# Quantising the last feed-forward's weights inside the preceding gated feed-forward, and a longer tile pipeline for the last one

## The chip, the cores and the metric

One NeuronCore of a Trainium2 chip runs one program. The metric is the device time of the program in microseconds (us); smaller is better. The engines are named as in the profile: PE is the matrix engine (PEld its weight loads), DVE the vector engine, ACT the scalar engine, POOL GpSimd, SP the engine that issues most of the DMAs.

## The reference, cut to what matters

Four layers, each an attention and a feed-forward with a residual, over an activation `x` of 4 x 512 x 256 in float32. The change touches the third layer's feed-forward (which keeps its own arithmetic), the start of the last attention, and the last feed-forward:

```python
# third layer's feed-forward, "L2_ffn": ternary weights, row scales s
h = silu(tlin(x, w1, s)) * tlin(x, w2, s)      # 256 -> 1024, gated
h = gelu(tlin(h, h1, s)); h = gelu(tlin(h, h2, s))   # 1024 -> 1024, twice
return tlin(h, w3, s)                          # 1024 -> 256

# last feed-forward, "L3_ffn": every operand is quantised to FP4 blocks
def fake_quant_nvfp4(x, global_scale):         # blocks of 16 along a row
    amax = max(abs(xb)); sc8 = fp8(clip(amax / 6 * global_scale, 0, 448))
    dq = sc8 / global_scale
    a = clip(abs(xb) / dq, 0, 6)
    return sign(xb) * nearest_fp4(a) * dq
def nvfp4_linear(x, w, s_in):
    s_w = 448 * 6 / max(abs(w))                # over the whole weight
    return fake_quant_nvfp4(x, s_in) @ fake_quant_nvfp4(w, s_w).T
hidden = silu(nvfp4_linear(x, gate_w, s_in)) * nvfp4_linear(x, up_w, s_in)
return nvfp4_linear(hidden, down_w, s_in_down)
```

`gate_w` and `up_w` are 1024 x 256, `down_w` is 256 x 1024.

## The kernel before

A Python program writes one list of steps, `plan`, and then five loops (one for each engine, `tensor_program`, `vector_program`, `scalar_program`, `gpsimd_program`, `sync_program`) walk that list; each engine takes its part of every step in the order of the list. So the place of a step in the list is its place in the queue of each engine that it uses. Waits are on semaphores, and `hold(latest_of_all(), ...)` at the end of a stage (`stage`) makes every engine wait for everything before.

**L2_ffn** works on two pairs of batches (1024 tokens each). For a pair it walks 40 weight blocks: 16 blocks of 256 x 128 for w1 and w2 in turn (the gated layer), 8 blocks of 1024 x 128 for h1, 8 for h2, and 8 for w3. `next_block` takes block n: it adds the split of block n+1 into a high and a low float32r part (`SplitBlock`: ACT copies the high part, L1916, DVE subtracts, L1761) and the load of block n+2 on SP. Then come the matmuls of the block (three passes, L1431) and a `HiddenTile` for each half of the tokens: ACT activation (L1919), in the gated layer DVE's product with the "up" half (L1765), ACT high copy (L1921), DVE low part (L1768). Two buffers each hold the raw blocks and the split ones. GpSimd does nothing in this stage, and the tile `XT` is unused.

**L3_xattn** begins with four weight loads and a 1 MB load of the context on SP, then a first batch's layer norm, whose square root stands in ACT's queue behind the copies of the turned context.

**L3_ffn** has two parts. First the weights: three loads of 1 MB and two scalars, then for gate, up and down in turn a `WeightScale` (DVE maximum of 128 x 2048, L1774; GpSimd `partition_all_reduce`, L2068; four tiny DVE operations), and the quantising of 128 x 2048 elements, whose result is turned by PE (16 transposes for each weight, L1588) and copied by ACT into `Gt`, `Ut`, `Dt` (bfloat16). A `hold` of all engines ends that part. Then the activations: `x_part(b)` normalises and quantises a batch (128 x 1024 elements), `hidden_part(t)` computes gate and up for a tile of 128 tokens (PE, ACT silu L1929, DVE product L1823), and `down_part(t)` quantises the hidden tile (128 x 1024), turns it, multiplies by `Dt` and adds to X (L1827), which is stored.

Quantising n elements is three pieces of work in the list. `Quantise`: DVE takes block maxima (L1787) and ten small operations in all on the n/16 block scales, each waiting for the one before, up to the inverse scales (L1807); then GpSimd multiplies the data by them (L2074). `RoundFp4`: DVE clips (L1811), masks the exponent (L1813), makes the grid step (L1816), adds and subtracts (L1818, L1820); then GpSimd multiplies by the scales into bfloat16 (L2082). `push` orders them so that the list has Quantise of item k, then RoundFp4 of item k-1, then the turning of item k-2. Two buffers hold y, q and the small scales; `Quantise` of item k waits for the GpSimd product of item k-2 (`y_free`). There is one `mg` buffer.

Of the kernel before, what the change touches and what calls it, by code (L numbers as in the profile page):

```python
# [8 lines left out]
P = 128  # L9
# [3 lines left out]
TB = S // P  # L13
# [111 lines left out]
WeightScale = namedtuple("WeightScale", "w col i s_in maxed reduced done")  # L125
Quantise = namedtuple("Quantise", "src n gs s after inv scaled")
RoundFp4 = namedtuple("RoundFp4", "s n after q_free rounded done")
# [16 lines left out]
def build_program(nc, dram, out):  # L144
    ctx = ExitStack()
    with ctx:
# [11 lines left out]
        def sem(event):  # L158
            return event.by.sem
# [48 lines left out]
        zero1 = sb(ctx, "zero1", [P, 1])  # L208

# [910 lines left out]
        def L2_ffn(scope):  # L1120
# [29 lines left out]
            n_block = [0]  # L1150

            def next_block():
# [74 lines left out]

            load_block(0)
# [5 lines left out]
            for pair in range(2):  # L1234
# [6 lines left out]
                e_out = output(pair, act[0], [e_h])  # L1241

# [17 lines left out]
        q4 = Stage()  # L1260

        def L3_ffn(scope):
            Gt, Ut = sb(scope, "L3f_GT", [P, KC, FF], BF16), sb(scope, "L3f_UT", [P, KC, FF], BF16)
            Dt = sb(scope, "L3f_DT", [P, KF, C], BF16)
            big = 2 * FF
            q4.y = [sb(scope, f"L3f_y{i}", [P, big]) for i in range(2)]
            q4.mg = sb(scope, "L3f_mg", [P, big])
            q4.qq = [sb(scope, f"L3f_q{i}", [P, big], BF16) for i in range(2)]
            q4.small = [sb(scope, f"L3f_small{i}", [P, 5, big // BLOCK]) for i in range(2)]
            col = sb(scope, "L3f_cols", [P, 12])  # L1270
            q_free, y_free, n_q = [None, None], [None, None], [0]

            def quantise(src, n, gs, after):
                s = n_q[0] % 2
                n_q[0] += 1
                st = Quantise(src, n, gs, s, [*after, y_free[s]], due("inverse_scales"), due("scaled"))
                add(st)
                return dict(s=s, n=n, read=st.scaled)

            def round_to_fp4(item):  # L1280
                s, n = item["s"], item["n"]
                st = RoundFp4(s, n, [item["read"]], q_free[s], due("fp4_rounded"), due("fp4_ready"))
                add(st)
                y_free[s] = st.done
                return s, q4.qq[s][:, 0:n], st.done

            half, whole = [], []

            def push(item, then):
                round_one()  # L1290
                half.append((item, then))

            def round_one():
                rounded = [(then, round_to_fp4(item)) for item, then in half]
                half.clear()
                for then, result in whole:
                    then(*result)
                whole[:] = rounded

            def flush():  # L1300
                round_one()
                round_one()

            def transposed(s, qo, pieces, dst, after, copy_after=()):
                for i in range(0, len(pieces), 4):
                    part = pieces[i:i + 4]
                    i_bank, bank = ALL.take()
                    st = Turn16(part, qo, bank.bitcast(BF16), [ALL.free[i_bank], *after], due("turned"), dst(i // 4),
                                list(copy_after), due("turned_out_scalar"))
                    add(st)  # L1310
                    ALL.free[i_bank] = st.done
                q_free[s] = st.mm
                return st.done

            with ExitStack() as inner:
                Wn = {n: sb(inner, f"L3f_{n}", [P, big]) for n in ("gate", "up", "down")}
                hold([
                    load(Wn["gate"][:, :].rearrange("p (m c) -> p m c", c=C), dram["L3_ffn_gate_w"].rearrange("(m p) c -> p m c", p=P)),
                    load(Wn["up"][:, :].rearrange("p (m c) -> p m c", c=C), dram["L3_ffn_up_w"].rearrange("(m p) c -> p m c", p=P)),
                    load(Wn["down"][:, :].rearrange("p (m c) -> p m c", c=FF), dram["L3_ffn_down_w"].rearrange("(m p) c -> p m c", p=P)),  # L1320
                    load(col[:, 10:11], dram["L3_ffn_s_in"].to_broadcast([P, 1])),
                    load(col[:, 11:12], dram["L3_ffn_s_in_down"].to_broadcast([P, 1]))])
                alpha = {}
                for i, (n, s_in) in enumerate((("gate", 10), ("up", 10), ("down", 11))):
                    g, al = col[:, 3 * i + 1:3 * i + 2], col[:, 3 * i + 2:3 * i + 3]
                    st = WeightScale(Wn[n][:, :], col, i, s_in, due("weight_max"), due("weight_max_all"), due("alpha_ready"))
                    add(st)
                    alpha[n] = al

# [846 lines left out]
```

## Time and profile before

| | us |
|---|---|
| median of three runs | 3914.71 (3909.6 to 3918.46) |
| the profiled execution | 3912.9 |
| its span in the trace | 3911.1 |
| DVE busy | 1951.7 (50%) |
| PE busy | 2835.9 (73%) |
| GpSimd busy | 1112.9 (28%) |

What lies around the span is 1.8 us. The rows are read so: a row of a timeline gives start, duration, engine, line, operation, output<-input with shapes, and in brackets the idle time of the engine before it and what ended it. A row of a table of windows gives the busy time of each engine in a stretch, with the number of instructions, the clock that PE was granted (1.00 is 2.4 GHz, 0.50 is 1.2 GHz), the busy share of the DMA engines and GB/s.

### The profile page before, as it was taken

The numbers are of one execution on the slowest core, as the hardware profiler recorded it, in microseconds if no ns is written. First come the engines' busy times: TensorE is split into PE (matmuls) and PEld (weight loads), VectorE is DVE, ScalarE is ACT, GpSimd is POOL, SyncE is SP. The second block draws the span as 40 slices with busy tenths as digits, with TensorE's granted clock in tenths as the row PEclk, the third lists the DMA queues.
The fourth block names the chain that finished last, engine by engine and source line by source line (L and its number), as shares of the span: only waits on it lengthen the run. The fifth ranks groups of instructions, "written<-read, shape, count | busy, mean of one in ns | idle before, by whom it ended". The sixth has DMA issues, their size and how long they took to land. (4 is left out here: it accounts for less than half of the span.)

```text
span 3911.1 us, 44194 instructions
## 1 busy us (share of the span) xinstructions
PE 2835.9 (73%) x16750; PEld 1614.4 (41%) x16756; DVE 1951.7 (50%) x3120; ACT 1478.5 (38%) x1967; POOL 1112.9 (28%) x989
## 2 busy tenths in 40 slices
PE   4899983668859389996837998478989967870243
PEld 2333332523336234443733444377877852320121
DVE  3554653556533634441664665453233226645797
ACT  1455553326622134542514555234323314650111
POOL 2132222113231235555024787400000011222232
PEclk7798996869969689998868999799999987995555
DMA  5354541045410001112010000001101124531000
GB/s 130 76 117 112 120 96 48 27 75 117 86 42 1 26 9 45 43 45 62 1 31 1 1 1 1 23 6 50 49 26 56 45 55 88 120 72 37 2 10 11
DMA packets 119730, 192.16 MB, mean 49 GB/s; under 512 B 33056, under 2 KB 57120, under 8 KB 119392
## 3 DMA queue, kind: packets, MB, share of 16 engines
q1 hardware_dynamic: 87776, 136.94, 15.3%
q0 software_dynamic: 31744, 52.41, 4.9%
q8 instruction: 134, 2.20, 0.3%
q14 instruction: 76, 0.62, 0.1%
HBM read 126.01 MB, written 63.18 MB: 48 GB/s over the span
## 5 line engine op out<-in xcount | busy, mean ns | idle before, releaser
L1676 DVE TENSOR_REDUCE L_mx<-bank_t 128x2 f32<-128x1024 f32 (+3 forms) x512 | 562.8, 1122 | 460.5 <-PE bank_t L1492 287.1
L1880 ACT ACTIVATE L_P<-bank_t 128x1024 f32<-128x1024 f32 (+2 forms) x512 | 477.8, 949 | 417.9 <-PE bank_t L1506 272.6
L1676 DVE TENSOR_REDUCE L2a_mx<-bank_t 128x2 f32<-128x1024 f32 x256 | 312.0, 1224 | 397.2 <-PE bank_t L1469 396.3
L1880 ACT ACTIVATE L2a_P<-bank_t 128x1024 f32<-128x1024 f32 x256 | 261.9, 1024 | 259.1 <-PE bank_t L1481 258.7
L1492 PE MATMUL bank_t<-L_KS,L_QS 48*128 48x512 f32 (+2 forms) x1024 | 255.3, 501 | 98.7 <-DMA L_QS<-L_spill_q_halves 76.3
L1506 PE MATMUL bank_t<-L_QS,L_KS 50*128 50x512 f32 (+2 forms) x1024 | 233.6, 459 | 90.3 <-DVE L_mx L1676 73.3
L1537 PE MATMUL bank_o<-L_P,L_V 128*32 128x512 f32 (+3 forms) x2048 | 274.0, 609 | 4.9 <-ACT xn L1887 3.3
L1492 PEld LDWEIGHTS bank_t<-L_KS,L_QS 48*128 48x128 f32 x1024 | 105.6, 205 | 341.7 <-issue 245.2
L1768 DVE TENSOR_TENSOR L2g_act_low<-ctxT,L2g_act_high 128x512 fp32r<-128x512 f32 x96 | 66.5, 693 | 291.9 <-ACT L2g_act_high L1921 291.9
L1442 PE MATMUL bank_t<-ident,xn 128*128 128x128 f32 x224 | 49.8, 394 | 218.2 <-DVE xn L1634 205.1
L1431 PE MATMUL bank_t<-L2g_act_high,L2g_w_high 128*128 128x512 f32 x480 | 190.0, 396 | 20.5 <-DVE L2g_w_low L1761 13.5
L1980 POOL MEMSET L_KS<- 32x2048 f32 x12 | 21.6, 1801 | 633.5 <-issue 604.7
L1431 PE MATMUL bank_t<-L2g_act_high,L2g_w_low 128*128 128x512 f32 x480 | 188.2, 392 | 0.0
L1431 PE MATMUL bank_t<-L2g_act_low,L2g_w_high 128*128 128x512 f32 x480 | 188.2, 392 | 0.0
L1993 POOL TENSOR_TENSOR L_lo<-L_full,L_hi 128x512 fp32r<-128x512 f32 x64 | 81.2, 1269 | 359.1 <-ACT L_hi L1867 348.1
L1506 PEld LDWEIGHTS bank_t<-L_QS,L_KS 50*128 50x128 f32 x1024 | 102.4, 198 | 186.6 <-DVE L_mx L1676 130.1
L1588 PE MATMUL bank_t<-ident,L3f_q 128*128 128x128 bf16 x152 | 19.7, 307 | 211.5 <-POOL L3f_q L2082 211.5
L1469 PE MATMUL bank_t<-L2a_K_high,L2a_Q_high 32*128 32x512 f32 x512 | 130.4, 506 | 46.7 <-ACT L2a_P L1880 27.6
L2003 POOL TENSOR_TENSOR L2a_sums<-L2a_sums,L2a_P 128x1024 f32<-128x1024 f32 x64 | 151.5, 2368 | 26.1 <-ACT L2a_P L1880 22.1
L1469 PEld LDWEIGHTS bank_t<-L2a_K_high,L2a_Q_high 32*128 32x128 f32 x512 | 52.9, 190 | 206.5 <-ACT L2a_P L1880 124.5
L1541 PE MATMUL bank_o<-L2a_P,ones 128*32 128x512 f32 x512 | 135.9, 608 | 0.0
L1442 PEld LDWEIGHTS bank_t<-ident,xn 128*128 128x128 f32 x224 | 39.8, 206 | 227.6 <-issue 130.4
(445 smaller groups left out, 6845.0 us busy)
## 6 DMA issues: line engine op xcount, KB each, us to landing
L_KS<-L_spill_k_halves SPq DMA_DIRECT2D x192, 128.0 KB, 4.2
L_QS<-L_spill_q_halves SPq DMA_DIRECT2D x192, 128.0 KB, 4.6
L_spill_raw<-xn POOLq DMA_DIRECT2D x64, 256.0 KB, 2.4
L2g_raw<-in_L_ffn_h_blocks SPq DMA_DIRECT2D x32, 512.0 KB, 3.4
L_spill_k_halves<-L_hi SPq DMA_DIRECT2D x32, 256.0 KB, 2.0
L_spill_k_halves<-L_lo SPq DMA_DIRECT2D x32, 256.0 KB, 2.3
L_spill_q_halves<-L_hi SPq DMA_DIRECT2D x32, 256.0 KB, 4.8
L_spill_q_halves<-L_lo SPq DMA_DIRECT2D x32, 256.0 KB, 5.2
```

What stands on the lines that cost most here:

```text
L1431: mm = e.matmul(out_, w, x, start=first and i == 0, stop=last and i == len(terms) - 1)
L1442: mm = e.transpose(s.bank[:, i * P:(i + 1) * P], tile, s.ident[:, :])
L1469: mm = e.matmul(m.tile[:, c, :], Q[r, m.qt * P:(m.qt + 1) * P], K[r, :], start=i == 0, stop=i == 2)
L1492: mm = e.matmul(m.tile[:, c, 0:n_keys], st.QS[m.un.buf][rows, slot, m.qt * P:(m.qt + 1) * P], st.KS[m.un.buf][rows, slot, 0:n_keys], start ...
L1506: mm = e.matmul(x.tile[:, c, q0:S], st.KS[x.un.buf][rows, slot, x.kt * P:(x.kt + 1) * P], st.QS[x.un.buf][rows, slot, q0:S], start=True, s ...
L1537: mm = e.matmul(bank_o[row:row + 32, q0:q1], V[:, s.kt, head, :], moving, start=s.first and i == 0, stop=s.last and i == len(cuts) - 1, ti ...
L1541: mm = e.matmul(bank_o[row + 32:row + 64, :], ones[:, 0:32], s.at.Pr[pb][:, c, :], start=s.first, stop=s.last, tile_position=(0, row + 32))
L1676: e.tensor_reduce(neg, s.tile[:, :, 0:n_keys], AX.X, ALU.max, negate=True).then_inc(sem(s.done), 1)
L1768: e.tensor_tensor(s.low, s.h, s.high.bitcast(F32), ALU.subtract).then_inc(sem(s.done), 1)
L1880: e.activation(s.at.Pr[s.pb][:, :, q0:S], s.tile[:, :, q0:S], ACT.Exp, scale=s.at.scale).then_inc(sem(s.exp), 1)
L1993: e.tensor_tensor(s.low[:, :], s.full, s.high[:, :].bitcast(F32), ALU.subtract).then_inc(sem(s.lo), 1)
L2003: e.tensor_tensor(s.dst[:, :, :], s.a[:, :, :], s.b[:, :, :], ALU.add).then_inc(sem(s.done), 1)
```

## The change

The three weights of the last feed-forward are quantised in L2_ffn by a generator, `quantised_weights`, of which `next_block` takes one step ahead of every block but those of w3 (64 blocks), and one step stands ahead of the stage. It works on twelve pieces of 128 x 512 elements (four to a weight) in buffers cut out of `XT`. In 15 steps it takes the maximum of each piece (`WeightMax`) and, after every fourth, a `WeightScale`. Then each piece takes three steps: in the first it is loaded again, `Quantise` and GpSimd's `ScaleBlocks`; in the second `GridSteps` and `RoundFp4`; in the third nothing. With the first step of the next piece it is turned (four transposes, one ACT copy) and stored to DRAM. Ahead of L3_xattn three loads bring `Gt`, `Ut`, `Dt` (1.5 MB in all) from DRAM. L3_ffn no longer has its first part.

`Quantise` and `RoundFp4` are split into `Quantise` (DVE, scales), `ScaleBlocks` (GpSimd), `GridSteps` (DVE, three operations) and `RoundFp4` (DVE add and subtract, GpSimd product). In L3_ffn the list is now, for item k: gate and up of item k+2 (with DVE's two products), `Quantise` of item k+1, the turning and down product of item k-2, then `ScaleBlocks`, `GridSteps` and `RoundFp4` of item k. The hidden tile has three buffers and `mg` two. Nineteen items go through it (batches 1 to 3 and 16 hidden tiles); batch 0 goes ahead of them by itself.

```diff
             def next_block():
                 n = n_block[0]
                 n_block[0] += 1
+                if blocks[n][0] != "w3":
+                    next(background, None)
                 split_block(n + 1)
                 load_block(n + 2)
...
+            next(background)
             load_block(0)
...
+        def quantised_weights():
...
+            ahead = [fetch(*pieces[0])]
+            yield
+            for i, (n, j) in enumerate(pieces):
+                ahead.append(fetch(*pieces[(i + 1) % 12]))
+                r, e_raw = ahead.pop(0)
+                st = WeightMax(maxes[:, i:i + 1], raw[r], [e_raw], due("piece_max"))
+                add(st)
+                raw_free[r] = st.done
+                yield
+                if j == 3:
+                    w = names.index(n)
+                    st = WeightScale(maxes[:, i - 3:i + 1], col, w, 10 if n != "down" else 11, [st.done, *e_in],
+                                     due("weight_max"), due("weight_max_all"), due("alpha_ready"))
                     add(st)
+                    fp4_ready[n] = st.done
+                    yield
+            item = None
+            for i, (n, j) in enumerate(pieces):
+                w = names.index(n)
+                if i + 1 < len(pieces):
+                    ahead.append(fetch(*pieces[i + 1]))
+                r, e_raw = ahead.pop(0)
+                item = quantise(q, raw[r], S, col[:, 3 * w + 1:3 * w + 2], [e_raw, fp4_ready[n]])
+                add(item["scale"])
+                raw_free[r] = item["read"]
+                yield
+                add(grid_steps(item))
+                s, qo, e = round_to_fp4(item)
+                yield
+                yield
...
+                e = transposed(q, s, qo, order, lambda _: staged[k].rearrange("p (j n) -> p j n", n=P), [e],
+                               [staged_free[k]])
...
+                add(Store(dst, src, [e], out_l))
...
-            for t in range(NT):
-                e_next = hidden_part(t + 1, x_ready[(t + 1) // TB]) if t + 1 < NT else None
-                down_part(t, e_hid)
-                if t % TB == 0 and t // TB + 1 < B:
-                    x_part(t // TB + 1)
-                e_hid = e_next
-            flush()
...
+            hidden_of(0)
+            hidden_of(1)
+            now, turning = scales_of(0), []
+            for k in range(len(work)):
+                hidden_of(k + 2)
+                coming = scales_of(k + 1)
+                if k >= 2:
+                    then, rounded = turning.pop(0)
+                    then(*rounded)
+                item, then = now
+                add(item["scale"])
+                add(grid_steps(item))
+                turning.append((then, round_to_fp4(item)))
+                now = coming
...
         stage(L2_ffn)
+        Gt, Ut = sb(ctx, "L3f_GT", [P, KC, FF], BF16), sb(ctx, "L3f_UT", [P, KC, FF], BF16)
+        Dt = sb(ctx, "L3f_DT", [P, KF, C], BF16)
+        for tile, n in ((Gt, "gate"), (Ut, "up"), (Dt, "down")):
+            load(tile[:, :, :], fp4_dram[n], fp4_stored)
         stage(L3_xattn)
-        stage(L3_ffn)
+        stage(lambda scope: L3_ffn(scope, Gt, Ut, Dt))
```

## Rows read from the trace of the kernel before

**Rows 1.** Windows by stage: busy us of each engine, PE clock, DMA share, GB/s.
```profile
core 0: us, PE busy (x) PEld busy (x) DVE busy (x) ACT busy (x) POOL busy (x), PEclk, DMA share, GB/s
2641.00:2700.00 59.00, 49.13 (x198) 37.99 (x199) 29.84 (x49) 28.99 (x50) 0.00 (x0) 0.96 0.19 56
...
2921.00:2973.00 52.00, 43.89 (x186) 33.88 (x184) 28.27 (x49) 26.14 (x47) 0.00 (x0) 1.00 0.20 58
2973.00:3155.00 182.00, 176.24 (x768) 145.16 (x768) 41.80 (x51) 58.87 (x82) 0.00 (x0) 0.99 0.13 42
...
3534.00:3631.00 97.00, 5.62 (x48) 4.88 (x48) 59.19 (x61) 6.20 (x12) 24.88 (x9) 0.51 0.10 33
...
3662.00:3901.00 239.00, 89.62 (x384) 45.92 (x387) 215.22 (x342) 38.56 (x66) 79.07 (x38) 0.59 0.03 9
```

**Rows 2.** Timeline, DVE, the last addition of L3_xattn to the first layer norm.
```profile
3531.96 0.69 DVE L1697 TENSOR_TENSOR X<-X,bank_m 128x512 f32<-128x512 f32 x1 [2.09 <-PE bank_m L1431]
3545.47 2.29 DVE L1774 TENSOR_REDUCE L3f_cols<-L3f_gate 128x1 f32<-128x2048 f32 x1 [12.82 <-DMA L3f_cols<-in_L_ffn_s_in_down]
...
3630.91 5.33 DVE L1612 BATCH_NORM_STATS2 stats<-X 128x6 f32<-128x256 f32 x16 [6.73 <-ACT L3f_DT L1925]
```

**Rows 3.** Timeline, SP, its first issue in L3_ffn.
```profile
3533.99 0.40 SPq L2099 DMA_DIRECT2D L3f_gate<-in_L_ffn_gate_w  x1
```

**Rows 4.** Timeline, DVE and POOL, one hidden tile and the next one's start.
```profile
3681.35 1.22 DVE L1787 TENSOR_REDUCE L3f_small<-L3f_hid 128x64 f32<-128x1024 f32 x1 [0.86 <-POOL L3f_q L2082]
...
3685.09 0.69 DVE L1811 TENSOR_SCALAR L3f_y<-L3f_y 128x1024 f32<-128x1024 f32 x1
3685.32 2.24 POOL L2074 TENSOR_TENSOR L3f_y<-L3f_hid,L3f_small 128x1024 f32<-128x1024 f32 x1 [4.07 <-DVE L3f_small L1807]
...
3685.81 2.30 DVE L1813 TENSOR_SCALAR L3f_mg<-L3f_y 128x1024 int32<-128x1024 int32 x1
...
3691.28 0.48 DVE L1827 SCALAR_TENSOR_TENSOR X<-bank_t,L3f_cols,X 128x256 f32<-128x256 f32 x1
3691.49 1.93 POOL L2082 TENSOR_TENSOR L3f_q<-L3f_y,L3f_small 128x1024 bf16<-128x1024 f32 x1 [3.93 <-issue]
3691.67 1.40 DVE L1823 SCALAR_TENSOR_TENSOR L3f_hid<-bank_t,L3f_cols,L3f_hid 128x512 f32<-128x512 f32 x2
...
3693.52 1.22 DVE L1787 TENSOR_REDUCE L3f_small<-L3f_hid 128x64 f32<-128x1024 f32 x1 [0.46 <-POOL L3f_q L2082]
```

**Rows 5.** Timeline, DVE, one period of the gated layer (pair 0).
```profile
2672.27 0.79 DVE L1761 TENSOR_TENSOR L2g_w_low<-L2g_raw,L2g_w_high 128x256 fp32r<-128x256 f32 x2
...
2678.79 0.78 DVE L1761 TENSOR_TENSOR L2g_w_low<-L2g_raw,L2g_w_high 128x256 fp32r<-128x256 f32 x2
2681.07 0.75 DVE L1765 SCALAR_TENSOR_TENSOR ctxT<-bank_t,L2g_scales,ctxT 128x512 f32<-128x512 f32 x1 [1.51 <-PE bank_t L1431]
```

**Rows 6.** Timeline, POOL, the first two all-reduces of L3_ffn.
```profile
3548.02 0.38 POOL L2068 PARTITION_ALL_REDUCE L3f_cols<-L3f_cols  x1 [22.77 <-DVE L3f_cols L1774]
...
3565.63 0.38 POOL L2068 PARTITION_ALL_REDUCE L3f_cols<-L3f_cols  x1 [6.03 <-issue]
```

**Rows 7.** Timeline, PE, first matmul of the first h1 block; windows, the ten us after.
```profile
2698.59 0.47 PE L1431 MATMUL bank_t<-L2g_act_high,L2g_w_high 128*128 128x512 f32 x1 [3.19 <-DVE L2g_act_low L1768]
...
2700.00:2710.00 10.00, 10.00 (x38) 8.07 (x38) 0.69 (x1) 1.32 (x2) 0.00 (x0) 0.83 0.18 54
```

**Rows 8.** The page's costliest groups: transposes of L3_ffn (busy us, mean ns | idle).
```profile
L1588 PE MATMUL bank_t<-ident,L3f_q 128*128 128x128 bf16 x152 | 19.7, 307 | 211.5 <-POOL L3f_q L2082 211.5
```

**Rows 9.** One line's instructions (ns min/median/max); timeline, a DVE reduction beside POOL.
```profile
L1688 DVE TENSOR_TENSOR L2a_mneg<-L2a_mx,L2a_mneg x32: 187/197/2400, 1390.2 to 2424.0; 128x16 fp32r<-128x16 f32 x32
...
3584.02 2.28 DVE L1774 TENSOR_REDUCE L3f_cols<-L3f_down 128x1 f32<-128x2048 f32 x1
3584.24 3.68 POOL L2082 TENSOR_TENSOR L3f_q<-L3f_y,L3f_small 128x2048 bf16<-128x2048 f32 x1 [7.14 <-DVE L3f_y L1820]
```

**Rows 10.** Timeline, PE, the turning of the context in L3_xattn.
```profile
3191.59 1.09 PE L1442 MATMUL bank_o<-ident,xn 128*128 128x128 f32 x4 [12.67 <-DMA xn<-in_ctx]
```

More of the change, by code:

```diff
@@ L1241, in L2_ffn @@
                 e_out = output(pair, act[0], [e_h])
+            assert next(background, "all done") == "all done"
         def L3_xattn(scope):
@@ L1258, in L3_xattn @@
                 Wq=Wq, Wk=Wk, Wv=Wv, bq=None, bk=None, bv=None, mode="full")], project_into(X, Wo), st, norm)
[L1260 to L1276, printed above, removed]
-                add(st)
[L1278 to L1282, printed above, removed]
-                add(st)
[L1284 to L1309, printed above, removed]
-                    add(st)
[L1311 to L1328, printed above, removed]
-                    def turn_weights(s, qo, e, n=n):
-                        if n == "down":
-                            for m in range(KC):
-                                transposed(s, qo, [m * FF + h * P for h in range(KF)],
-                                           lambda j, m=m: Dt[:, 4 * j:4 * j + 4, m * P:(m + 1) * P], [e])
-                        else:
-                            Wt = Gt if n == "gate" else Ut
-                            for k in range(KC):
-                                transposed(s, qo, [m * C + k * P for m in range(KF)],
-                                           lambda j, k=k, Wt=Wt: Wt[:, k, 4 * j * P:(4 * j + 4) * P].rearrange(
-                                               "p (j n) -> p j n", n=P), [e])
-                    push(quantise(Wn[n][:, :], big, g, [st.done]), turn_weights)
-                flush()
-                hold(latest_of_all(), ("sync", "tensor", "vector", "scalar", "gpsimd"))
@@ new lines, in build_program, with quantise @@
+        fp4_dram = {n: nc.dram_tensor(f"L3f_{n}_fp4", shape, BF16, kind="Internal").ap()
+                    for n, shape in (("gate", [P, KC, FF]), ("up", [P, KC, FF]), ("down", [P, KF, C]))}
+        fp4_stored, fp4_ready = [], {}
+        def quantise(q, src, n, gs, after):
+            s = q.count % 2
+            q.count += 1
+            e_inv, e_scaled = due("inverse_scales"), due("scaled")
+            add(Quantise(q, src, n, gs, s, [*after, q.y_free[s]], e_inv))
+            return dict(q=q, s=s, n=n, read=e_scaled, scale=ScaleBlocks(q, src, n, s, [e_inv], e_scaled))
@@ new lines, in transposed @@
+        def transposed(q, s, qo, pieces, dst, after, copy_after=()):
+            for i in range(0, len(pieces), 4):
+                part = pieces[i:i + 4]
+                i_bank, bank = ALL.take()
+                st = Turn16(part, qo, bank.bitcast(BF16), [ALL.free[i_bank], *after], due("turned"), dst(i // 4),
+                            list(copy_after), due("turned_out_scalar"))
+                add(st)
+                ALL.free[i_bank] = st.done
+            q.q_free[s] = st.mm
+            return st.done
@@ new lines, in L3_ffn @@
+        def L3_ffn(scope, Gt, Ut, Dt):
+            big = FF
+            alpha = {n: col[:, 3 * i + 2:3 * i + 3] for i, n in enumerate(("gate", "up", "down"))}
+            q4 = quantiser([sb(scope, f"L3f_y{i}", [P, big]) for i in range(2)],
+                           [sb(scope, f"L3f_mg{i}", [P, big]) for i in range(2)],
+                           [sb(scope, f"L3f_q{i}", [P, big], BF16) for i in range(2)],
+                           [sb(scope, f"L3f_small{i}", [P, 5, big // BLOCK]) for i in range(2)])
@@ L1784, in vector_program @@
                     nb = s.n // BLOCK
-                    am, sc8, M, inv, e8 = (q4.small[s.s][:, i, 0:nb] for i in range(5))
+                    am, sc8, M, inv, e8 = (s.q.small[s.s][:, i, 0:nb] for i in range(5))
                     dve.wait_ge(*s.after)
```

132 lines of the change are left out of this document (103 added, 29 removed).

## The prediction

> **What bounds the kernel now.** I first read the windows by stage. L2_ffn has two gated layers of some 55 us, in which PE is busy 44 to 49 us and DVE 28 to 30 [rows 1], and the 1024-wide layers, in which PE is busy 176 of 182 us and DVE 42. GpSimd is idle in all of it. The weight part of L3_ffn takes 97 us with PE nearly idle and DVE at 59. Its tile part takes 239 us, of which DVE is busy 215. So L3_ffn is DVE's and GpSimd's, the 1024-wide layers are PE's, and the gated layer is neither's: it is a chain through engines. The timeline shows where the weight part lies: from the last addition of L3_xattn, which ends at 3532.6, through SP's first issue at 3534.0 [rows 3], to the first layer norm at 3630.9 [rows 2].
>
> One hidden tile takes 3693.52 - 3681.35 = 12.17 us [rows 4]: DVE's scale chain 3.74 (to the clip at 3685.09), the clip 0.72, the mask 2.3, step, add and subtract 3.1, the down product 0.4, the gate products 1.4, and 0.46 idle until GpSimd's product of 3691.49 is out. The mask has as many elements as the clip, which takes 0.69, and is 2.30 because GpSimd is at work from 3685.32 to 3687.56.
>
> **The change, part by part.**
>
> *The weight part goes.* In the changed kernel the layer norm can begin where SP begins now: 3630.9 - 3534.0 = 97 us off, all on the path.
>
> *The tile pipeline.* For item k DVE has the gate products, the scales of item k+1, the down product, then clip, mask, step, add, subtract. GpSimd starts the final product of item k-1 when DVE's subtract ends (t = 0): it is out at 0.14 + 1.93 = 2.1. The gate products (1.4) run beside it, as at 3691.67 now, at their full speed. The block maxima of item k+1 wait for that product (the small scales are shared with item k-1), so they start at 2.2. GpSimd scales item k from 2.2 to 4.1, beside the maxima; a reduction isn't slowed by GpSimd (2.28 us beside a product of 3.68 us [rows 9]) and ends at 3.4. The small operations then wait until 4.1: a tiny DVE operation with two inputs in SBUF, 0.20 at the median, took up to 2.40 [rows 9], and the mask shows the same of a TENSOR_SCALAR. The chain, 3.74 long plus 0.6 of this wait, ends at 6.5; down product 0.4; clip, mask, step 3 x 0.72; add and subtract 2.4: 11.5 us. So the mask's 1.6 us is won and about 0.9 us of it given back, 0.65 a tile, times 19 items = 12. Two batches normalised inside the loop meet GpSimd's second product and lose some 0.5 each: 11 us off. Ends: nothing (the small operations all held as the mask is now), and 19 x 1.6 = 30 less the overlap of products, 20.
>
> *The background in the gated layers.* A period, 2672.27 to 2678.79, is 6.52 us [rows 5]. It is a chain: up matmuls, DVE product, ACT copy, twice, then the split of the next "up" block: DVE's w_low, and PE. The low part of the second half and the w_low stand back to back on DVE, and PE waits for it. Of two background steps in a period, one stands right ahead of that w_low and is paid in full; the other stands ahead of the split of the next gate block, and behind that DVE idles 1.51 us [rows 5], so 1.5 us of it is covered.
> Prices, DVE: `WeightMax` of 512 elements, half of 1.22: 0.65. `Quantise` of a piece: 0.65 and nine small operations that take 3.74 - 1.22 = 2.5 at 64 blocks; between all and half of that at 32, I take 2.1, because 0.2 us each is mostly fixed: 2.75. `GridSteps` and `RoundFp4` of 512: 0.72 x 3 + 2.4 = 4.6 at 1024, so 2.3 or a little over: 2.75. `WeightScale`: reduction, an all-reduce of 0.38 with 0.3 around it, four tiny operations: 1.7.
> Pair 0 has steps 2 to 17: in the paid place six maxima and two WeightScales (3.9 + 3.4), in the covered one a WeightScale and the first Quantise over 1.5 (0.2 + 1.2): 8.7. The all-reduce had 6.03 us of issue ahead of it where a GpSimd product came before it, and none where GpSimd had only waited [rows 6]; here no product stands between the three, so I cost that at nothing. If not, two more times 6: 12.
> Pair 1 has steps 34 to 49, with work in ten. Paid place: three roundings and two Quantises, 13.8. Covered place: three Quantises over by 1.2 and two roundings over by 1.2, these also waiting 1.1 us for GpSimd's scaling, which is too near: 3.6 + 4.6. Together 22.
> PE's gap between periods is now about 1.2 us; with a step of 2.75 it is 4. After a gap of 3.19 the clock stood at 0.83 over the next ten us, that is some 3.4 us at the lower level [rows 7]. Five such times, mostly over matmuls with slack, 0.6 each: 3. If all of the lower stretch told, 1.7 each and the next gap too: 15.
>
> *The background in the 1024-wide layers.* A block is 48 matmuls, about 11 us (768 in 182 us); DVE has 41.8 / 16 = 2.6 us of its own in it and gets under 3 more: hidden behind PE [rows 1]. What lands on PE are the turns: 12 groups of four transposes, five of them in the gated layer's gaps. A transpose is 0.307 us, pipelined, at the lower clock [rows 8], so a group is 0.3 to 0.6 us: 7 x 0.5 = 3.5. ACT has 58.9 / 16 = 3.7 us in a block, so its copy of 0.6 or so has room.
>
> *SP and the DMAs.* Ahead of the stage's first block stand three more issues, of 0.4 us each [rows 3], and 256 KB; DVE and ACT wait for that block: 2. In the stage each turn's store waits for ACT on SP, and the next block's load stands behind it; at 11 us a block this is covered, in the gated layer it is inside the paid 2.75.
> Ahead of L3_xattn stand three issues and 1.5 MB, in front of the context, for which PE waits 12.67 us [rows 10]. Now 3 MB take from 3534.0 to 3545.4, 11.4 us, so 1.5 MB take about 5: 5 us on. Ends: 0 and 9. The Trainium skill ("SBUF — State Buffer", The DMA setup-cost knee) gives 2 us and bytes over 436 GB/s, by which 1.5 MB behind others would add 3.6, and the sum would be 1.4 less. No row here shows so high a rate.
>
> **The sum**: -97 - 11 + 8.7 + 22 + 3 + 3.5 + 2 + 5 = -64. Against the profiled 3912.9 this gives 3849; the median of before is 1.8 above that execution, and I take 3850. A difference below 0.2% (8 us) can't be told from none here.
>
> **The rivals.**
> *The gated layers take the background almost free* (0.13). For it: DVE is busy only 30 of 59 us there. Against it: the idle time stands behind the wrong waits [rows 5]. The 31 us become about 8, the tile part gives 15: 3822.
> *The shared port makes it dearer* (0.17). Every weight split and low part of L2_ffn is a DVE subtraction of two SBUF inputs, and 24 new GpSimd products of 1.06 us (half of 1.93 and a little) can stand in front of one; that is the mechanism of the 2.40 us [rows 9]. If all of them told, +25; with the clock's 12 more: 3887. I expect most to fall into DVE's idle time, and the likeliest price is half: about 3870. The Trainium skill says so of `tensor_tensor` with two SBUF inputs and of GpSimd operations that read SBUF ("SBUF — State Buffer", Who interferes with whom), and that a reduction never contends; both agree with rows 9.
> *The tile pipeline gives nothing* (0.08), because the scales are held to the end of GpSimd's second product: +11, 3861; it lies in my own range.
> *Slower* (0.03). SP is one queue: a block's load stands behind the store of a turned piece, which waits for POOL, PE and ACT. If the loads came a block late, each of the 12 turns would cost PE up to a block of 11 us, 132 together, and the kernel would end at 3849 + 132 = 3981. It decides from 64 / 12 = 5.3 us a turn. Against it: the piece is turned two blocks, 22 us, after its rounding is issued, and a load has a whole block to land in.
> *That the change does not do what it says* (0.01): loads of `Gt` and the others wait for the last store, and the last turn falls to step 53 of 65, so they are not held.
>
> **How the numbers follow.** The forecast with its own spread has 0.58. Its range, from the ends of the unknown costs that are not likely all at once, is 3835 to 3866. With the two rivals around it the range of 8 in 10 is 3818 to 3884. Faster by over 0.2%: 0.96; within: 0.01; slower: 0.03.
>
> **What would show it.** The window between L3_xattn's last addition and the first layer norm of L3_ffn shrinks from 98 to 1 or 2 us. L1813 of 1024 elements falls from 2.30 to 0.69, the first small operation after the maxima (L1790) takes about 0.6 us more than now, and a tile takes 11.5. The gated layer of pair 0 grows by 9 and that of pair 1 by 25, with PE waiting for w_low (L1761); the 1024-wide layers grow by 0.5 a turn; PE's wait for the context grows by 5. I am wrong if pair 1's gated layer grows by under 12 or over 40, if DVE's small operations run freely beside GpSimd, or if PE has gaps in the 1024-wide layers.

## The result, and the profile after

The changed kernel takes 3855.08 us (3839.35 to 3871.86, four runs) against 3912.49 for the kernel before in the same series: a ratio of 0.9852, interval 0.9808 to 0.9895, so it is faster by some 1.5%. A second series gave 3863.24 against 3919.58, ratio 0.9846 (0.9814 to 0.9878). The forecast was 3850, range 3818 to 3884. The profiled execution took 3871.86 us, its span is 3869.9.

The windows by stage, changed kernel: each gated layer from its first to its last product on DVE, the 1024-wide layers and w3 behind it, L3_xattn from addition to addition, and the tile part of L3_ffn. They answer to [rows 1]; line numbers are now 79 to 85 higher.

```profile
core 0: us, PE busy (x) PEld busy (x) DVE busy (x) ACT busy (x) POOL busy (x), PEclk, DMA share, GB/s
2662.05:2718.84 56.79, 43.38 (x169) 33.00 (x167) 37.75 (x80) 23.70 (x44) 1.67 (x4) 0.94 0.34 100
2718.84:2945.45 226.61, 209.72 (x1006) 176.53 (x1007) 88.86 (x195) 68.95 (x103) 20.69 (x12) 0.95 0.15 46
2949.44:3023.19 73.75, 50.24 (x188) 37.05 (x186) 52.77 (x110) 25.19 (x48) 10.46 (x10) 0.86 0.21 62
3023.19:3231.79 208.60, 199.76 (x964) 168.42 (x964) 54.98 (x88) 62.67 (x91) 3.82 (x2) 0.99 0.14 42
3231.79:3599.98 368.19, 254.83 (x1248) 99.56 (x1248) 183.61 (x226) 171.43 (x204) 77.19 (x94) 0.80 0.45 92
3603.35:3869.90 266.55, 97.56 (x409) 47.02 (x416) 210.79 (x402) 44.93 (x75) 77.22 (x40) 0.57 0.02 8
```

The same stretch of a gated layer before, in windows of the kernel before:

```profile
2648.48:2697.01 48.53, 40.25 (x169) 30.81 (x168) 27.45 (x45) 23.74 (x44) 0.00 (x0) 1.00 0.21 61
2924.77:2973.35 48.58, 40.12 (x169) 30.81 (x167) 27.41 (x45) 23.75 (x44) 0.00 (x0) 1.00 0.20 59
```

The gated layers grew from 48.5 to 56.8 and from 48.6 to 73.7 us: 8.3 and 25.2, where the prediction has 9 and 25. DVE got 10.3 us more work in the first and 25.4 in the second, and the first is longer by most of it, the second by all of it. The stretches of the 1024-wide layers and w3 take 2.2 and 0.3 us more.

The waits of PE in the gated layer of pair 1, the longest before and the longest changed:

```profile
2929.57 0.47 PE L1431 MATMUL bank_t<-L2g_act_high,L2g_w_high 128*128 128x512 f32 x1 [1.91 <-DVE L2g_w_low L1761]
```

```profile
2956.94 0.77 PE L1510 MATMUL bank_t<-L2g_act_high,L2g_w_high 128*128 128x512 f32 x1 [4.86 <-DVE L2g_w_low L1840]
```

Before, the six other periods of that layer have a wait of 0.81 to 0.83 us there. With the change it is over 4 us three times, and it is still DVE's w_low that ends it.

The timeline of DVE where L3_ffn begins, changed kernel (answers to [rows 2]):

```profile
3599.29 0.69 DVE L1776 TENSOR_TENSOR X<-X,bank_m 128x512 f32<-128x512 f32 x1 [2.09 <-PE bank_m L1510]
3603.35 5.32 DVE L1691 BATCH_NORM_STATS2 stats<-X 128x6 f32<-128x256 f32 x16 [3.38 <-issue]
```

The first layer norm came 98.3 us behind the last addition and now comes 3.4 behind it: 94.9 us are gone.

The timelines of DVE and POOL for one hidden tile, changed kernel (answers to [rows 4]):

```profile
3790.00 1.22 DVE L1867 TENSOR_REDUCE L3f_small<-L3f_hid 128x64 f32<-128x1024 f32 x1 [0.84 <-POOL L3f_q L2167]
3791.25 0.70 DVE L1870 TENSOR_SCALAR L3f_small<-L3f_small,L3f_cols 128x64 f32<-128x64 f32 x1
...
3795.29 0.69 DVE L1893 TENSOR_SCALAR L3f_mg<-L3f_y 128x1024 int32<-128x1024 int32 x1
...
3799.15 1.40 DVE L1908 SCALAR_TENSOR_TENSOR L3f_hid<-bank_t,L3f_cols,L3f_hid 128x512 f32<-128x512 f32 x2
3801.39 1.22 DVE L1867 TENSOR_REDUCE L3f_small<-L3f_hid 128x64 f32<-128x1024 f32 x1 [0.85 <-POOL L3f_q L2167]
...
3789.97 1.93 POOL L2159 TENSOR_TENSOR L3f_y<-L3f_hid,L3f_small 128x1024 f32<-128x1024 f32 x1
3799.36 1.93 POOL L2167 TENSOR_TENSOR L3f_q<-L3f_y,L3f_small 128x1024 bf16<-128x1024 f32 x1 [7.46 <-issue]
```

A tile takes 3801.39 - 3790.00 = 11.39 us in place of 12.17 (11.5 forecast). The mask (L1893) is 0.69 and was 2.30; DVE now waits 0.85 for GpSimd's product in nearly every tile (0.46 in most of them before, 0.85 in some); and the first small operation behind the maxima (L1870) takes 0.70 and took 0.25. It ends at 3791.95, when GpSimd's product of 3789.97 ends at 3791.90.

DVE and POOL in the gated layer of pair 1, changed kernel:

```profile
2955.77 0.69 DVE L1902 TENSOR_TENSOR XT<-XT 128x512 f32<-128x512 f32 x1
2956.38 1.61 DVE L1840 TENSOR_TENSOR L2g_w_low<-L2g_raw,L2g_w_high 128x256 fp32r<-128x256 f32 x2
...
2968.84 0.43 DVE L1891 TENSOR_SCALAR XT<-XT 128x512 f32<-128x512 f32 x1 [0.95 <-POOL XT L2159]
...
2956.59 1.12 POOL L2167 TENSOR_TENSOR XT<-XT 128x512 bf16<-128x512 f32 x1 [6.71 <-issue]
```

Two w_lows took 0.79 us together [rows 5]; here, with GpSimd's product in front of the second, 1.61. The clip of a piece waits 0.95 us for GpSimd's scaling (1.1 forecast). The start of L3_xattn on PE and SP, changed kernel:

```profile
3244.66 3.65 PE L1521 MATMUL bank_t<-ident,xn 128*128 128x128 f32 x16 [15.64 <-DMA xn<-in_ctx]
...
3232.16 0.33 SPq L2184 DMA_DIRECT2D L3f_GT<-L3f_gate_fp  x1
```

PE waits 15.64 us for the context, 12.67 before [rows 10].

### The profile page after: what moved, and what is told of

Read it like the earlier page. It is cut to its first block and busy times, and to the rows that moved or that the text cites. A ratio compares the mean times of both kernels' runs of the same rounds, so it can differ in the third digit from the quotient of the medians.

```text
span 3869.9 us, 44492 instructions
## 1 busy us (share of the span) xinstructions
PE 2867.2 (74%) x16749; PEld 1621.9 (42%) x16756; DVE 1942.0 (50%) x3267; ACT 1476.8 (38%) x1967; POOL 1117.9 (29%) x1007
## 5 line engine op out<-in xcount | busy, mean ns | idle before, releaser
L1571 PE MATMUL bank_t<-L_KS,L_QS 48*128 48x512 f32 (+2 forms) x1024 | 264.4, 519 | 109.7 <-DMA L_QS<-L_spill_q_halves 87.9
L1616 PE MATMUL bank_o<-L_P,L_V 128*32 128x512 f32 (+3 forms) x2048 | 282.4, 627 | 4.9 <-ACT xn L1972 3.4
L1521 PE MATMUL bank_t<-ident,xn 128*128 128x128 f32 x220 | 48.8, 395 | 222.0 <-DVE xn L1713 193.2
L1585 PEld LDWEIGHTS bank_t<-L_QS,L_KS 50*128 50x128 f32 x1024 | 105.8, 205 | 184.1 <-DVE L_mx L1755 127.5
L1616 PE MATMUL bank_o<-L2a_P,L2a_V 128*32 128x512 f32 (+3 forms) x896 | 132.3, 527 | 0.2 <-ACT L2a_P L1965 0.2
L2083 POOL TENSOR_TENSOR L2a_diag<-L2a_P,after_q 128x256 f32<-128x256 f32 x128 | 93.4, 730 | 134.1 <-issue 75.6
```

The lines of the kernel that those rows point to most:

```text
L1521: mm = e.transpose(s.bank[:, i * P:(i + 1) * P], tile, s.ident[:, :])
L1571: mm = e.matmul(m.tile[:, c, 0:n_keys], st.QS[m.un.buf][rows, slot, m.qt * P:(m.qt + 1) * P], st.KS[m.un.buf][rows, slot, 0:n_keys], start ...
L1585: mm = e.matmul(x.tile[:, c, q0:S], st.KS[x.un.buf][rows, slot, x.kt * P:(x.kt + 1) * P], st.QS[x.un.buf][rows, slot, q0:S], start=True, s ...
L1616: mm = e.matmul(bank_o[row:row + 32, q0:q1], V[:, s.kt, head, :], moving, start=s.first and i == 0, stop=s.last and i == len(cuts) - 1, ti ...
L2083: e.tensor_tensor(s.dst[:, :, :], s.src, after_q[:, :].unsqueeze(1).to_broadcast([P, 2, P]), ALU.mult).then_inc(sem(s.done), 1)
```

## The experiments

Twelve runs follow, four of them of kernels without an edit. Medians of kernels of different series move by several us, and so do parts of the kernel that no edit touches, so most readings below are stage lengths in the profiles. The marks are DVE's last addition into X ahead of a stage, the first and last product of each gated layer, and in L3_xattn PE's first "stacked" matmul, that is the first product of `L_KS` and `L_QS` (us):

| profile | ahead of L2_ffn | its start | gated, pair 0 | wide, pair 0 | gated, pair 1 | wide, pair 1 | L3_xattn to its first stacked matmul | from there to its end | L3_ffn |
|---|---|---|---|---|---|---|---|---|---|
| before | 2617.8 | 30.7 | 48.5 | 224.4 | 48.6 | 208.3 | 45.3 | 305.7 | 378.4 |
| changed | 2629.4 | 32.7 | 56.8 | 226.6 | 73.7 | 208.6 | 50.1 | 318.1 | 269.9 |
| e1 changed again | 2618.7 | 32.8 | 56.9 | 226.4 | 73.8 | 208.7 | 49.8 | 313.0 | 270.0 |
| e2 h only | 2606.8 | 33.3 | 48.5 | 225.9 | 48.5 | 213.4 | 50.2 | 316.2 | 270.0 |
| e3 old tiles | 2624.3 | 32.7 | 56.8 | 226.5 | 73.8 | 208.6 | 50.6 | 314.1 | 285.1 |
| e4 narrow products | 2630.1 | 33.3 | 56.3 | 226.5 | 71.3 | 210.2 | 50.3 | 317.9 | 270.3 |
| e5 before again | 2634.2 | 31.0 | 48.5 | 224.3 | 48.6 | 209.9 | 43.3 | 312.4 | 378.3 |
| e6 three sets | 2637.0 | 33.4 | 56.9 | 227.3 | 73.8 | 211.3 | 50.6 | 305.3 | 268.9 |
| e7 loads last | 2624.0 | 33.4 | 56.9 | 227.3 | 73.8 | 211.4 | 46.8 | 323.8 | 270.0 |
| e8 steps at w2 | 2621.5 | 32.2 | 48.8 | 227.9 | 53.1 | 211.3 | 50.2 | 313.6 | 270.0 |
| e9 steps at w1 | 2625.4 | 33.4 | 54.7 | 227.2 | 64.4 | 211.5 | 50.6 | 313.1 | 270.1 |
| e10 all together | 2607.6 | 31.3 | 48.5 | 225.6 | 48.5 | 213.3 | 46.5 | 308.9 | 268.8 |
| e11 before, third | 2623.1 | 30.8 | 48.5 | 224.4 | 48.5 | 208.3 | 45.2 | 305.9 | 377.9 |
| e12 before, fourth | 2610.1 | 30.7 | 48.5 | 224.5 | 48.5 | 208.4 | 45.1 | 310.0 | 379.6 |

(Between the two pairs lie another 3.3 us, or 4.0 to 4.9 with steps there.)

**The changed kernel again (e1).** No edit.

> The changed kernel once more, for the spread of its stages. Theory: the 17 us by which L3_xattn was longer (368 against 351 us) are 3 us of a later start and the rest TensorE's clock, which wanders from run to run; then the stages ahead of L2_ffn and L3_xattn move by up to 15 us against the first profile, while L2_ffn (602 us) and L3_ffn (270 us) stay within 4. Rival: something that the change leaves behind slows L3_xattn; then it takes 365 us or more again. Median 3855 either way, between 3845 and 3865.

Measured: 3863.24 us. L2_ffn and L3_ffn repeat within 0.2 us. The code ahead of L2_ffn, the same in both, is 10.7 us shorter than in the first profile, L3_xattn 5.4. The median is inside the 3845 to 3865 that were expected. So these two stages vary between executions; whether the change also adds to them, this run leaves open (see e5, e11, e12).

**No step in the gated layers (e2).**

```diff
-                if blocks[n][0] != "w3":
-                    next(background, None)
+                if blocks[n][0] in ("h1", "h2"):
+                    next(background, None)
+                    next(background, None)
```

> No background step in the gated layers, two in each block of the 1024-wide layers. Theory (the gated layer is a chain through DVE, the 1024-wide layer is PE's): the gated layers return to their 52 to 55 us, so 9 to 13 us in pair 0 and some 25 in pair 1 are won, and the 1024-wide blocks of 11 us hide both steps but for the turns' 0.5 us: 3855 - 34 = 3821 (3815 to 3828). Rival 1: DVE's 2.6 us and two steps of 2.75 with GpSimd's products do not fit in front of the next block's split, PE gets gaps: 3835 to 3850. Rival 2: the growth of L2_ffn came from loads and stores on SP, not from DVE: it moves along with the steps, 3850.

Measured: 3829.64 us, ratio to before 0.9765 (0.9731 to 0.9798), 34 less than the changed kernel in the same series, as expected, and the time is 1.6 us above the expected range of 3815 to 3828. Windows of e2, gated layers, then the 1024-wide layers of each pair:

```profile
2640.10:2688.60 48.50, 40.32 (x170) 30.90 (x168) 27.48 (x45) 23.73 (x44) 0.00 (x0) 1.00 0.18 57
2917.80:2966.30 48.50, 40.38 (x173) 31.03 (x171) 27.43 (x45) 23.73 (x44) 0.00 (x0) 1.00 0.17 52
2688.60:2914.40 225.80, 208.65 (x1006) 175.29 (x1007) 102.07 (x231) 69.04 (x103) 19.86 (x15) 0.95 0.19 62
2966.30:3179.70 213.40, 204.73 (x984) 171.69 (x984) 81.80 (x162) 65.22 (x96) 20.45 (x12) 0.98 0.17 51
```

Both gated layers are at 48.5 again. All twelve pieces now stand in the 1024-wide layers and cost there 1.5 and 5.1 us over before; over twelve turns that is 0.55 us each. (The stretch of pair 1 took 208.6 us in some profiles of the changed L2_ffn and 211.3 in e6 and e7, with the same instructions, so this price is good to some 0.3 us a turn.) DVE's second row has 81.80 us in 213 and PE is busy 204.73: the work is hidden. Rival 1 falls, and rival 2 as it was put (3850). But the loads and stores of the background moved along with its steps, so that they cost nothing in the gated layers either is not shown by this run.

**The old order of the tiles (e3).**

```diff
-            first, turn_first = x_part(0)
...
+            push(*x_part(0))
+            flush()
+            e_hid = hidden_part(0, x_ready[0])
+            for t in range(NT):
+                e_next = hidden_part(t + 1, x_ready[(t + 1) // TB]) if t + 1 < NT else None
+                push(*down_part(t, e_hid))
+                if t % TB == 0 and t // TB + 1 < B:
+                    push(*x_part(t // TB + 1))
```

> Weights in the background as in the changed kernel, L3_ffn's tiles in the order of the kernel before (scaling added right behind the scales, rounding one item behind). Theory: a tile takes 12.17 us again, its mask 2.30 and its first small operation 0.25, and the time is 11 us over the changed kernel's: 3866. From the profile (tiles at 11.4 us against 12.17, 19 items) 13 to 15 are also possible. Rival, the longer pipeline gives nothing: 3855.

Measured: 3881.66 us, 18 over the changed kernel in the same series (11 to 15 expected), and L3_ffn 285.1 against 270.0: the pipeline gives 15.1 us. DVE and POOL in e3:

```profile
3774.45 0.69 DVE L1886 TENSOR_SCALAR L3f_y<-L3f_y 128x1024 f32<-128x1024 f32 x1
3775.17 2.30 DVE L1888 TENSOR_SCALAR L3f_mg<-L3f_y 128x1024 int32<-128x1024 int32 x1
...
3774.68 2.24 POOL L2154 TENSOR_TENSOR L3f_y<-L3f_hid,L3f_small 128x1024 f32<-128x1024 f32 x1 [4.07 <-DVE L3f_small L1882]
```

The mask is 2.30 again. Between additions into X a tile takes 12.17 us here and 11.41 in e1. Thirteen tiles by 0.76 make 10; four tiles with a batch between them went from 61.9 to 58.9 us, which is the four tiles' share alone. The last four additions span 19.7 us instead of 24.7: 5 more, at the end of the loop.

**GpSimd's background products narrowed (e4).** Both products work on 16 of 512 elements, so that the rest of the quantised weights stays zero, and a memset of their targets is added on idle GpSimd.

```diff
+                    n_ = s.n if s.n == FF else BLOCK
-                    e.tensor_tensor(blocks(s.q.y[s.s][:, 0:s.n]), blocks(s.src),
+                    e.tensor_tensor(blocks(s.q.y[s.s][:, 0:n_]), blocks(s.src[:, 0:n_]),
```

> Each of the background's two GpSimd products is made on one block of 16 elements in place of 512 (the rest of the quantised weights is left at zero, so the output is not the reference's; a memset of 2 us on idle GpSimd is added at the start). DVE's instructions, the turns, loads and stores stay. Theory: the gated layers' growth is DVE's own instructions; GpSimd costs only the three w_lows of 1.6 to 2.4 us and the waits of 0.95 us: 5 to 8 us less, 3848. Rival, the shared port makes the growth: 15 to 25 less, 3835. Rival, it costs nothing: 3855.

Measured: 3871.46 us where 3848 was expected; the ratio of 0.9853 (0.9817 to 0.9888) is not to be told from the changed kernel's 0.9846, so the reading rests on the stage lengths. The gated layers are 0.5 and 2.5 us shorter, the 1024-wide layers of pair 1 1.6 longer, which is within what that stretch varies by. GpSimd's share of the 33.5 us is about 3, less than the 5 to 8 of the theory, and the rival of the shared port falls.

**The two places in the gated layer (e8, e9).** One step in front of only every second block there; two in each 1024-wide block. e8 has "w2" in the first line, e9 "w1".

```diff
-                if blocks[n][0] != "w3":
+                if blocks[n][0] in ("w2", "h1", "h2"):
+                    next(background, None)
+                if blocks[n][0] in ("h1", "h2"):
                     next(background, None)
```

> In the gated layers a background step only ahead of the split of the next gate block (the place behind which DVE idles 1.5 us), two steps in each 1024-wide block. Theory, the place decides: pair 0 has eight steps of 0.65 there, which are covered, 48.5 us as before the change (56.8 with it); pair 1 has eight of which three are scale steps and two or three roundings, over by 1.2 each: 55 us (73.8 with the change). Time 3 to 9 us over the kernel that takes no step in the gated layers. Rival, DVE's time counts wherever it stands: pair 0 48.5 + 8 x 0.65 = 53.7, pair 1 48.5 + 5.3 x 2.75 = 63.

> The mirror of the steps at the other place: in the gated layers a background step only ahead of the split of the next up block, behind which PE waits for w_low, two steps in each 1024-wide block. Theory, this is the place that is paid in full: pair 0 takes 48.5 + 8 x 0.65 = 53.7 us (48.8 at the other place), pair 1 48.5 + 5 or 6 x 2.75 = 62 to 65 (53.1 at the other place), L2_ffn 15 us longer than there: 591, and the time 3849. Rival, the two places are alike: 577 and 3834.

Measured: e8 3833.81 us (ratio 0.9784, 0.9758 to 0.981), e9 3845.32 (0.9833, 0.9803 to 0.9863). Windows of e8, gated layers of pair 0 and 1:

```profile
2653.70:2702.50 48.80, 40.29 (x170) 30.88 (x168) 31.41 (x56) 23.65 (x45) 0.38 (x1) 1.00 0.31 96
2926.00:2979.10 53.10, 44.55 (x197) 33.73 (x196) 37.44 (x82) 22.83 (x44) 5.57 (x5) 1.00 0.18 52
```

The same of e9:

```profile
2658.80:2713.50 54.70, 41.91 (x170) 32.03 (x168) 31.68 (x56) 23.60 (x44) 0.38 (x1) 0.97 0.26 82
2945.80:3010.20 64.40, 48.39 (x186) 36.60 (x184) 39.33 (x75) 24.81 (x46) 4.45 (x4) 0.89 0.18 54
```

Against the 27.4 us of DVE before, e8 adds 4.0 us of DVE work in pair 0 and loses 0.3; e9 adds 4.2 and loses 6.2. In pair 1, 10.0 us more work cost 4.5 at the one place, 11.9 cost 15.8 at the other. L2_ffn of e9 is 19.4 us longer than that of e8 (15 expected). The place decides. At the paid one the loss is larger than the work itself; there the granted clock was 0.97 and 0.89 over the two layers (1.00 in e8), and PE had waits of up to 3.4 us, as the table of PE's waits in pair 1 shows. For e8 (us in total, times, longest):

```profile
PE bank_t L1512 <- DVE L2g_w_low L1842: 7.3, 7, 1.6
```

and for e9:

```profile
PE bank_t L1512 <- DVE L2g_w_low L1842: 10.5, 5, 3.3
PE bank_o L1512 <- DVE L2g_w_low L1842: 3.8, 2, 3.4
```

Could the loads on SP have done it? A late load reaches PE through ACT's high copy and DVE's w_low. In pair 0 of the changed kernel and of e9 no high copy waits for a load, and yet 8.3 and 6.2 us were lost. In pair 1 of the changed kernel the high copy waits for one twice, for 3.6 us and here for 4.1:

```profile
2968.88 0.42 ACT L2001 ACTIVATE L2g_w_high<-L2g_raw 128x256 fp32r<-128x256 f32 x1 [4.10 <-DMA L2g_raw<-in_L_ffn_w_blocks]
```

but DVE was at a background step until 2971.56 and took the w_low at once; no w_low of that layer waits for ACT. So late loads happened and were hidden behind DVE. In pair 1 of e9, w_low did wait for the high copy, 3.8 us in four times, so there a part of the 15.8 us may be the loads'.

**Three sets of buffers in L3_ffn (e6).**

```diff
-            s = q.count % 2
+            s = q.count % len(q.y)
...
-            q4 = quantiser([sb(scope, f"L3f_y{i}", [P, big]) for i in range(2)],
+            q4 = quantiser([sb(scope, f"L3f_y{i}", [P, big]) for i in range(3)],
```

> The changed kernel with three sets of small scales, products and halves in L3_ffn, so that the block maxima of an item need not wait for GpSimd's product of the item before (0.85 us idle in each of 19 items). Theory, the small operations wait for the port that GpSimd's second product holds: the maxima start 0.8 us earlier, the first small operation behind them grows from 0.70 to 1.5 us, and L3_ffn stays at 269 to 270 us. Rival, they run freely beside GpSimd and the 0.85 us are won: 19 x 0.85 = 16 less, L3_ffn 254.

Measured: 3869.74 us, L3_ffn 268.9 in place of 270.0, as the theory had it. DVE and POOL in e6:

```profile
3754.28 1.21 DVE L1867 TENSOR_REDUCE L3f_small<-L3f_hid 128x64 f32<-128x1024 f32 x1
3755.53 1.65 DVE L1870 TENSOR_SCALAR L3f_small<-L3f_small,L3f_cols 128x64 f32<-128x64 f32 x1
3757.20 0.20 DVE L1872 TENSOR_SCALAR L3f_small<-L3f_small 128x64 f32<-128x64 f32 x1
...
3755.19 1.93 POOL L2159 TENSOR_TENSOR L3f_y<-xn,L3f_small 128x1024 f32<-128x1024 f32 x1
```

The maxima start with no idle time, and all of it comes back in L1870: 1.65 us, until 3757.18, when GpSimd's product ends at 3757.12. A tile stays at 11.4. This is the term "small operations wait for GpSimd" alone, and it holds. The Trainium skill ("SBUF — State Buffer", Who interferes with whom) says that DVE in its two-port modes and GpSimd share a pair of ports, which the first to issue holds for its whole instruction, and that a reduction does not take part; the 1.21 of the reduction and the 1.65 of the operation behind it agree with that. Whether the small operation runs in such a mode no row shows.

**The loads of Gt, Ut and Dt behind L3_xattn's plan (e7).**

```diff
-        for tile, n in ((Gt, "gate"), (Ut, "up"), (Dt, "down")):
-            load(tile[:, :, :], fp4_dram[n], fp4_stored)
         stage(L3_xattn)
```

(the two lines stand at the end of `L3_xattn` instead.)

> The changed kernel with the loads of Gt, Ut and Dt issued behind the whole of L3_xattn's plan instead of ahead of it. Theory, they stand in front of the context and the weights: PE's wait for the context is 12.7 us again, its first stacked matmul comes 45.3 us after the last addition of L2_ffn and not 50.2, L3_xattn takes 5 us less than the 363 to 368 of the kernels with the change, that is 358 to 363, and L3_ffn starts no later, since the loads have PE's last 20 us to land: 5 us less. Rival, the loads shift the whole stage's clock too: 350 to 354. Rival, they make L3_ffn late instead: its start grows by the 5 us that they take.

Measured: 3874.91 us where 5 us less than the changed kernel was expected. PE in e7:

```profile
3240.26 3.64 PE L1521 MATMUL bank_t<-ident,xn 128*128 128x128 f32 x16 [12.28 <-DMA xn<-in_ctx]
```

The wait is back at 12.28, the first stacked matmul comes after 46.8 us instead of 50.1, and L3_ffn is not later: 3.3 of the 4.8 us are won. The rest of the stage took 323.8, the longest of all, so L3_xattn as a whole went the other way than both theories, and the total shows nothing.

**The kernel before, three more times (e5, e11, e12).** No edit.

> The kernel before once more, with a profile. L3_xattn took 351 us in its one profile and 363 to 368 in the five of kernels with the change, of which its later start (PE's first stacked matmul 5 us later) explains 5. Theory A, the rest is TensorE's clock that wanders: L3_xattn of this run is 355 to 362 us. Theory B, the change slows the attention itself by another 10 us: 349 to 353 again. L2_ffn 564, L3_ffn 378.5, within 1.

> The kernel before, a third profile. In the two so far L3_xattn took 351.0 and 355.7 us, in eight kernels with the change 355.9 to 370.6, 5 of it by the start. Theory A, the rest is the clock's wander: this one lies above 356. Theory B, the change also slows the body of the attention: again 350 to 356.

> As the third profile of the kernel before: above 356 us of L3_xattn speaks for the wander of the clock, 350 to 356 in all four for a slower body of the attention with the change (its body, behind the 167th microsecond, took 184 and 193 us before, 188 to 204 with the change).

Measured: L3_xattn 355.7, 351.1 and 355.1 us. With the first profile that is 351 to 356 in four, against 355 to 371 in ten profiles with the change. Behind the first stacked matmul the kernel before takes 305.7 to 312.4 (mean 308.5), the others 305.3 to 323.8 (mean 314.4). The ranges overlap and the means are 5.9 apart. By what was laid down ahead of each, e5 fell on the side of wander (355 to 362), e11 and e12 on that of a slower body of the attention. Two of the ten (e6, e10) are as fast as the kernel before. (For the part behind the 167th microsecond the last expectation has 193 us in e5; by these marks it is 188.7.) No edit here isolates a cause, and it stays open.

**All that helped, together (e10).** The edits of e2, e6 and e7, and the first background load behind the first norm:

```diff
-            next(background)
             load_block(0)
...
...
             xt = norm_pair(0, None)
+            next(background)
```

> No step in the gated layers and two in each 1024-wide block, the loads of Gt, Ut and Dt behind L3_xattn's plan, three sets of scales, and the first background load behind the first norm of L2_ffn. Theory: L2_ffn 573 - 2.5 = 570.5, its start 30.8 us; L3_xattn's first stacked matmul 46.8 us after L2_ffn; L3_ffn 269: 3830 - 2.5 - 3.4 - 1 = 3823, between 3815 and 3832 as TensorE's clock wanders. Rival, what is won at the starts is lost in the clock: 3830.

Measured: 3817.15 us (3804.38 to 3821.26), ratio to before 0.9752 (0.9729 to 0.9774): inside the expected 3815 to 3832 and 2.5% faster than before; the changed kernel's ratios in its two series are 0.985. L2_ffn starts 2.0 us earlier than in e2, L3_xattn's first stacked matmul 3.7 earlier, L3_ffn is 268.8.

## Why the prediction was right, step by step

*The weight part, -97.* 94.9 measured. DVE starts 3.4 us behind the last addition and not 1.4 as SP did; 2 us were missed.

*The tile pipeline, -11.* -15.1 (e3 against e1). The tile was right: 11.4 for 11.5, with the mask, the wait for the product and the wait of the small operation each within 0.2 us of the row. The size was off by the end of the loop, which the step did not look at: the last four additions are 5 us closer together; why, no run isolates. The 15.1 is the upper end: behind the first layer norm L3_ffn took 280.2 to 281.7 us in the four profiles of the kernel before, 281.8 in e3 and 266.6 in the changed kernel, so the pipeline gives 13.6 to 15.1. The 0.5 feared for a batch normalised in the loop showed, and more: four tiles and a batch went from 61.9 to 58.9 us, which is 0.75 for each tile and nothing for the batch, where the step gave the batch 0.65 less 0.5.

*Gated layers, 8.7 and 22, with 3 for the clock.* 8.3 and 25.2. That the steps make it is shown by e2 (gone when they go), and that it goes by the place by e8 and e9; that it is DVE's work and not a late load, by the waits of ACT and of w_low in the trace, for pair 1 of e9 only in part. The six us around an all-reduce did not come, as DVE's row behind the first one shows:

```profile
2674.68 0.16 DVE L1856 RECIPROCAL L3f_cols<-L3f_cols 128x1 f32<-128x1 f32 x1 [0.67 <-POOL L3f_cols L2153]
```

*The clock, +3.* Not separable as a term: the granted clock stood at 0.94 and 0.86 in the two layers, 1.00 before. The same 169 matmul records of pair 0 kept PE busy 3.1 us longer (43.38 against 40.25), and in pair 1 it was 10.1 us for 19 more; the prediction had five short stretches, all in pair 1, and 3 us (PE's gap in a period of before is 0.8 us and not the 1.2 that it took). What part of this lay on the chain no run isolates, so it is in part luck that the layers' sum came out at 33.5 for 33.7: the division between DVE's work and the clock is not shown. That e9 lost 1.3 to 1.5 us for each us of added DVE work, at 0.97 and 0.89, and e8 less than half a us at 1.00, fits a share of the clock.

*Turns in the 1024-wide layers, +3.5 for seven.* +2.5 in the two stretches and 0.7 between them, where a step now stands; e2 with all twelve gives 0.55 each, 0.5 forecast. In e6 and e7, whose L2_ffn is the changed kernel's, the two stretches are 5.9 over the first profile of before, so the term is known to some 3 us.

*Start of L2_ffn +2, start of L3_xattn +5.* 2.0 and 4.8. Of the second, 3.0 is the wait for the context [rows 10]. The rest is not the loads', since e7, which moves them, keeps 1.5 of it (46.8 against 45.3 us); most of it is a wait of PE for a copy by DVE (0.98 us ahead of the keys' product) that the kernel before does not have. An estimate by bytes and rate as in the Trainium skill ("SBUF — State Buffer", The DMA setup-cost knee) is 3.6; the wait alone grew by 3.0 over before and by 3.4 over e7, nearer to that than to the 5 from the row. That the term came out at 4.8 is luck: 3 to 3.4 from the loads, and 1.5 that the prediction did not have.

The terms as measured between the first two profiles, with L3_ffn as a whole (378.4 to 269.9, as the two terms above overlap by the spread just named): -108.5 + 8.3 + 25.2 + 3.2 + 2.0 + 4.8 = -65.0, against -64 in the forecast. That the terms add up so closely is in part luck: the weight part gave 2 us less, the pipeline some 3 to 4 more. The medians fell by 57.4 and 56.3. Some 8 us are therefore lost outside the terms, and the only stage where the profiles show a loss is the rest of L3_xattn (5.9 in the means). The prediction had no term for it. Its time was 5 us off and not 7, because the median of the kernel before was 2 us lower in this series than the 3914.7 it started from.

*The rivals.* "Almost free" fell: 33.5 us in the gated layers. "The shared port makes it dearer" fell by e4: 3 us. "The pipeline gives nothing" fell by e3. SP held no block back by a block's length: the 1024-wide layers grew by 2.5 us in all, not 132.

## What to carry to other kernels

In this kernel background work was nearly free only where the engine that carries it would have idled anyway, or where the stage was bound by another engine. Count idle time by the place in the engine's order, not by busy share: here the same 4 us of DVE work cost 0.3 us in front of one block and 6.2 in front of the next, and none that the runs show in the layers bound by PE, where only the turns on PE cost (0.55 us each). When a wait is taken away beside a shared port, look for the next instruction that needs the port before counting it as won.

## What the runs showed of the hardware

- A small DVE operation of 128x64 elements, 0.25 us alone, took 0.70 or 1.65 us beside GpSimd and ended within 0.06 us of GpSimd's product, while the reductions in front of it kept their 1.21 to 1.22 us.
- Stages vary with nothing changed in them: the code ahead of L2_ffn took 2607 to 2637 us in fourteen profiles, and L3_xattn 356 to 368 in the eight with the loads of `Gt`, `Ut` and `Dt` ahead of it, while L3_ffn repeated within 0.4 us in the seven profiles that leave it as changed (269.9 to 270.3).
- The body of L3_xattn takes longer where the granted clock is lower. In the four profiles of the kernel before, with nothing changed, the part behind the 167th microsecond took 184.0 and 184.1 us at a granted clock of 0.93 (before and e11), 188.1 at 0.90 (e12) and 188.7 at 0.88 (e5). With the change it was 195.8 us at 0.92 in e1 and 203.6 at 0.83 in e7, which differ only in where three loads stand; these windows hold up to 5 us more of the attention than those of before, since it starts later in the stage. e1:

```profile
3388.28:3584.07 195.79, 147.12 (x846) 57.53 (x839) 96.38 (x102) 112.50 (x129) 48.66 (x68) 0.92 0.43 90
```

and e7:

```profile
3397.70:3601.30 203.60, 157.10 (x822) 59.68 (x820) 93.36 (x99) 109.39 (x125) 47.08 (x65) 0.83 0.40 92
```

PE is busy 10 us longer in e7 for 24 matmul records fewer. What sets the clock lower in one execution than in another stays open.
